# A graph layer and a gated feed-forward layer on one core: seven loads of weights and biases change their issuing engine and their place

## What is computed

```python
edge_index = jnp.stack([src, dst])          # 200000 edges, sorted by dst; 12500 nodes, 256 features
x = x + gnn(_layernorm(x), edge_index, W, att_src, att_dst, bias)
x = x + ffn(_layernorm(x)[None], mask, wr, br, w1, b1, w2, b2)[0]

def gnn(x, ...):                            # 4 heads of 64
    xp = (x @ W).reshape(n, H, C)
    a_src = einsum(xp, att_src); a_dst = einsum(xp, att_dst)
    alpha = leaky_relu(a_src[src] + a_dst[dst], 0.2)      # edges and self loops
    w = softmax of alpha over the edges of each dst
    return elu(segment_sum(xp[src] * w, dst) + bias)

def ffn(x, ...):                            # hidden width 1024
    weights = x @ wr + br;  pick the half of the rows with the largest weights
    y = (gelu(x[picked] @ w1 + b1) @ w2 + b2) * weights[picked]
    return x + y at the picked rows
```

## Time and profile before

| | us |
|---|---|
| median of 3 executions | 2301.69 |
| lowest and highest | 2298.26 and 2302.06 |
| the profiled execution | 2303.54 |
| its span in the profile | 2301.8 |

### The profile page before, as it was taken

The page is one execution under the profiler, slowest core; times in us unless marked ns, Lnnn a source line. Parts: engine busy times, 40 slices in busy tenths (PEclk is TensorE's granted clock), DMA queues, the critical chain, the costliest instruction groups (busy, mean ns, idle before and its releaser), DMA issues.

```text
span 2301.8 us, 39185 instructions
## 1 busy us (share of the span) xinstructions
PE 1900.7 (83%) x10810; PEld 1660.8 (72%) x10811; DVE 1608.2 (70%) x3952; ACT 707.3 (31%) x1868; POOL 1592.7 (69%) x1675
## 2 busy tenths in 40 slices
PE   5955888888888988888889888888889888888881
PEld 4844777777777777777777777777778677777771
DVE  5756767667776776667666766777667677777668
ACT  3530323322332333223322332233323332333230
POOL 2257777777777777777777777777777777777700
PEclk9977898899899899999989989989999899999985
DMA  7745545555555555555555555555545555555458
GB/s 238 222 137 147 152 143 154 158 143 149 158 154 142 155 153 158 145 148 159 153 146 150 155 157 144 149 158 153 156 141 152 159 148 144 158 155 157 132 170 296
DMA packets 216112, 365.40 MB, mean 159 GB/s; under 512 B 62165, under 2 KB 151409, under 8 KB 216082
## 3 DMA queue, kind: packets, MB, share of 16 engines
q0 software_dynamic: 77488, 214.85, 33.8%
q1 hardware_dynamic: 121570, 134.31, 18.4%
q10 hardware_dynamic: 17024, 15.90, 2.0%
HBM read 326.04 MB, written 38.89 MB: 159 GB/s over the span
## 4 chain that ended last, share of the span: by engine, by line
POOL 55%; issue 23%; PE 8%; POOLq 6%; DVE 4%; DMA 2%; ACTq 1%; ACT 1%; SPq 0%; DVEq 0%
POOL rows L611 55%; POOLq L365 3%; PE ag_ps L800 3%; PE ag_ps L910 3%; DVE base L1398 2%; DMA rows<-node_rows,ends 2%; POOLq L627 2%; PE y_ps L891 1%; PE h_ps L878 0%; DVE rows L1210 0%; PE tr_ps L823 0%; PE xl_ps L823 0%; DMA steps_of_rows<-in_L_gnn_att_dst 0%; DVE st_b L1016 0%; ACTq L657 0%
## 5 line engine op out<-in xcount | busy, mean ns | idle before, releaser
L611 POOL DMA_INDIRECT rows<-node_rows,ends x1613 | 1552.5, 963 | 504.0 <-issue 489.8
L910 PE MATMUL ag_ps<-rows,oh 128*128 128x260 f32 x3322 | 914.9, 443 | 291.1 <-DVE rows L1210 291.1
L910 PEld LDWEIGHTS ag_ps<-rows,oh 128*128 128x128 f32 x3322 | 731.3, 224 | 444.8 <-issue 298.4
L1210 DVE TENSOR_TENSOR rows<-rows,xl_ps 128x768 f32<-128x768 f32 (+2 forms) x685 | 495.7, 793 | 38.5 <-ACT xl_ps L731 38.5
L878 PE MATMUL h_ps<-xnT,w1s 128*128 128x128 f32 x3136 | 366.8, 275 | 0.0
L878 PEld LDWEIGHTS h_ps<-xnT,w1s 128*128 128x128 f32 x3136 | 358.2, 192 | 11.2
L731 ACT ACTIVATE xl_ps<-diff 128x68 f32<-128x68 f32 x98 | 22.6, 231 | 1109.9 <-DVE diff L1199 1099.4
L891 PE MATMUL y_ps<-w2s,hT 128*128 128x256 f32 x1568 | 359.6, 383 | 3.2 <-ACT hT L713 3.2
L1191 DVE TENSOR_TENSOR zz<-rows,edge_dm 128x68 f32<-128x68 f32 x98 | 22.4, 229 | 470.6 <-DMA rows<-node_rows,ends 373.2
L891 PEld LDWEIGHTS y_ps<-w2s,hT 128*128 128x128 f32 x1568 | 299.9, 192 | 45.2 <-issue 3.5
L1172 DVE TENSOR_TENSOR oh<-xl_ps,dloc 128x2176 f32<-128x2176 f32 x98 | 236.9, 2418 | 0.0
(11 more groups left out here) (183 smaller groups left out, 1329.6 us busy)
## 6 DMA issues: line engine op xcount, KB each, us to landing
dbc<-dst SPq DMA_DIRECT2D x97, 544.0 KB, 4.9
rows<-node_rows,ends POOLq DMA_INDIRECT x1613, 2.7
selfr<-node_rows SPq DMA_DIRECT2D x98, 130.0 KB, 2.1
base<-in_x SPq DMA_DIRECT2D x14, 896.0 KB, 5.2
base<-in_x SPq DMA_DIRECT2D x49, 256.0 KB, 2.8
ffn_rows<-yb ACTq DMA_DIRECT2D x96, 128.0 KB
node_rows<-base SPq DMA_DIRECT2D x13, 910.0 KB, 5.8
out<-base SPq DMA_DIRECT2D x3, 1024.0 KB, 6.1
```

Of the source, the lines that this page charges most:

```text
L611: pool.indirect_dma_start(out=rows[:, b, t, :], out_offset=None, in_=table, in_offset=bass.IndirectOffsetOnAxis(ap=ends[:, b, t, 0:1], axi ...
L910: product = nc.tensor.matmul(ag_ps[b][:, 0:ROW], oh[:, b, t, :], rows[:, b, t, :], start=(t == 0), stop=False)
L1210: nc.vector.tensor_tensor(v, v, e, ALU.mult).then_inc(scaled[k], 1)
```

## The change

The seven issues leave ScalarE's stream, where they stood ahead of its first copy. They stand now in SP's stream, in `batch_io(10)`, behind the store of batch 9 and ahead of that of batch 10. Their order, shapes, destinations and semaphores are the same, and no wait is added ahead of them.

```diff
+            def load_weights():
+                sp.dma_start(bias_f[0], bc(b2, D)).then_inc(b2_ld, 16)
+                sp.dma_start(gbs[:, :], bc(gbias, D)).then_inc(w_ld, 16)
+                sp.dma_start(w1s[:, :, :], w1.rearrange("(c p) n -> p c n", p=P)).then_inc(w_ld, 16)
+                sp.dma_start(w2s[:, :, :], w2.rearrange("(c p) n -> p c n", p=P)).then_inc(w_ld, 16)
+                with nc.allow_non_contiguous_dma("a bias by column of the hidden layer"):
+                    sp.dma_start(b1s[:, :], b1.rearrange("(c p) -> p c", p=P)).then_inc(w_ld, 16)
+                sp.dma_start(wrs[:, :], bc(wr.rearrange("d o -> (d o)"), D)).then_inc(w_ld, 16)
+                sp.dma_start(brs[:, :], bc(br, 1)).then_inc(w_ld, 16)
...
                 if known(g, 1):
                     store_rows(g - 1, 1 - b)
+                if isinstance(g, int) and g == NB - DEEP:
+                    load_weights()
...
-            act.dma_start(bias_f[0], bc(b2, D)).then_inc(b2_ld, 16)
-            act.dma_start(gbs[:, :], bc(gbias, D)).then_inc(w_ld, 16)
-            act.dma_start(w1s[:, :, :], w1.rearrange("(c p) n -> p c n", p=P)).then_inc(w_ld, 16)
-            act.dma_start(w2s[:, :, :], w2.rearrange("(c p) n -> p c n", p=P)).then_inc(w_ld, 16)
-            with nc.allow_non_contiguous_dma("a bias by column of the hidden layer"):
-                act.dma_start(b1s[:, :], b1.rearrange("(c p) -> p c", p=P)).then_inc(w_ld, 16)
-            act.dma_start(wrs[:, :], bc(wr.rearrange("d o -> (d o)"), D)).then_inc(w_ld, 16)
-            act.dma_start(brs[:, :], bc(br, 1)).then_inc(w_ld, 16)
```

## The result

| | us |
|---|---|
| kernel before, median of 5 (2296.31 to 2302.06) | 2298.26 |
| changed kernel, median of 5 (2285.30 to 2288.71) | 2287.04 |
| ratio, with its 95% interval | 0.9942 (0.9932 to 0.9953) |
| forecast for the changed kernel | 2289.3 |

The changed kernel is faster: by the ratio 0.58%, by the two medians 11.2 us, which is 0.49%; both lie inside the interval. The forecast was 12.4 us, 0.54%. Two further executions of the kernel before brought its median down by 3.4 us against the three that the forecast started from, so the gain is a little smaller than forecast while the time is 2.3 us lower. The profiled execution of the kernel before (2303.54 us) lies 5.3 us above that median. Measured again beside the first group of experiments, the same kernel has a ratio of 0.9947 (0.9933 to 0.9961), 11.6 us.

What follows compares the result with a forecast made beforehand. Stage two's GpSimd gathers fill over half the chain; the first waits for stage one's last table store. Terms -12.4 and 0 took 2303.54 to 2291.1 us, less 1.85 to the median: 2289.3 us, range 2285 to 2294.

Steps and rivals of the forecast that it cites:

- The main term: Front of stage one: without the seven issues on ScalarE, TensorE's first product comes at about 14.5 us, not 26.91; -12.4 us.
- D: Rival, chance 0.04: transfers pace the start, so moving the issues wins only their own 3.2 us; 2298.5 us.
- A: Rival, chance 0.09: the 6.12 us hold follows the 127 pieces and falls on ScalarE's copy; gain 9.4 us, 2292.3 us.
- cost nothing: Behind the first product: batch 1's normalization, target conversion, later loads and the moved loads on SP delay nothing; 0 us.
- the cover of batch 1: VectorE's normalized tiles, coming since 21.8 us, are ready before TensorE needs them at 25.3 us; about 3.5 us of cover.
- Loads of later batches are issued by the progress of the work itself and move with it.: Loads behind batch 3's were claimed to come earlier along with the work, at no cost.
- The clock: 0: TensorE's first products, 3.05 us lost to slow running, were taken to stay as slow after the change; gain 0.
- C: Rival, chance 0.05: TensorE's clock comes up sooner at its first products, winning up to 3.05 us more; 2286.3 to 2288 us.
- The price on SP: Seven issues behind batch 9's store take 3.4 to 15.5 us, taken towards the lower; term 0, range 0 to +1.5 us.
- B: Rival, chance 0.08: SP is held long and its queue is full, delaying batch 10's store; 2291 to 2292.5 us.
- E: Rival, chance 0.02: SP held some 53 us or more makes the last table stores late; at 55 us, about 2308 us.
- a microsecond of stage one shows up in the total: Stage one lies wholly ahead of the first gather, so each microsecond on its chain counts in the total if nothing gives it back.

Runs made afterwards that it cites:

- first group of experiments: The changed kernel, unaltered, measured again as the base for that group's other kernels: 2288.95 us, ratio 0.9947 to the kernel before.
- third group: The last set of executions, all programs some 900 us longer; its base, the changed kernel unaltered: 3225.46 us, ratio 0.9972 to the kernel before.

## Why the prediction was right, and where it was not

**The reading of the bound was right.** The first gather waits for the last store before and after. The main term too: the first copy was held by the seven issues. It was forecast to start at 14.0 us and started at 13.55, the first product at 14.07 for 14.5. Of that 0.36 us is an earlier landing of the attention vector in this execution (the first issue stands at 9.52 us, not 9.88). Term -12.4, measured -12.84. That SP issues from the same early place give most of the gain rules D out. A is out since in the changed kernel the copy starts 0.03 us after its tile is ready (12.86 + 0.66 = 13.52 us), 3.1 us behind the issue of the 127 pieces.

**The step that failed: "cost nothing" for everything behind the first product.** By the prediction's own sign (a new idle time of TensorE on VectorE's normalization before 40 us) this part is wrong. Two of its terms failed, the cover of batch 1 and the time of the store of batch 0.

*The cover at batch 1.* The prediction gave 3.5 us; by its own lead it was 0.9, and in this profile there was none. It took the mean of 3.97 us for each of the seven and had the first tile ready at 21.8 us, but the first operation was 2.0 us long and the others 0.4, so the tile was ready at 22.9 us. It also had TensorE come for it at 25.3 us, behind the seventh product, though the transposes of the eighth tile stand ahead of that product: by the forecast's lead at 36.24 - 12.4 = 23.8 us, and with the fast first steps of this profile at 22.05, where it waited 0.90 us. This wait cost next to nothing against the kernel before, which waits 0.84 us at this place for ScalarE's conversion of the targets: the eighth product is 38.57 - 24.33 = 14.24 us ahead, the ninth 39.78 - 25.44 = 14.34, as the fourth was (33.12 - 18.77 = 14.35).

*"Loads of later batches are issued by the progress of the work itself and move with it."* This was wrong for one load. The load of batch 5 waits for the normalization of batch 1, which VectorE does in its own time: its issue is at 25.26 us before and 24.90 us after. The store of batch 0 moved from 38.87 to 25.39 us and so came to stand 0.5 us behind it, in the same queue. It took 9.1 us to land, against 4.2 before, and ScalarE waited 1.89 us at batch 2, a term that the prediction did not have; in this pair of profiles 1.11 us of the lead were lost there.

**The clock: 0 is not refuted, and it is not shown.** In the pair of profiles above 1.5 us were won in TensorE's first three steps, which looks like the prediction's C. The other profiles take that back. With the change or a variant of it the three steps took 4.70, 4.69, 5.95, 5.63, 5.95, 5.46, 4.92, 5.74 and 5.04 us. Without it, behind the long wait, they took 6.21 us in the kernel before and 29.85 - 25.04 = 4.81 us with the 127 pieces moved. The two ranges lie over each other, so no gain by C is shown. TensorE idles for some 10 us ahead of its first transposes in either kernel, and only products put into a wait made the first tile fast (1.06 to 1.13 us for four).

These two findings are not independent. Where the first steps were fast, ScalarE waited for the store of batch 0; where they were slow (5.95 us, changed kernel of the third group), it came later and did not wait. The store of batch 2 was issued at 41.57, 41.94 and 41.63 us in the three profiles of the changed kernel, with first steps of 4.70, 4.69 and 5.95 us: what fast steps win, the wait takes back.

**The price on SP was right in effect and wrong in size.** The prediction took a value towards 3.4 us and named 3.4 to 8 us; the seven took 10.3 us. The outer bounds of 3.4 and 15.5 us held. The reason given, that the DMA engines are idle there (0.02), was read from a stretch of the kernel before, without the weights. With them the share was 0.86 from 97 to 101 us and 0.99 from 101 to 107. SP alone did not pay the lower bound either, so two queues that hold each other up are not the whole cause of the hold. With b1 last the longest hold fell to 1.5 us at a share of 0.82 to 0.85, so most of it belongs to the issue that follows the pieces of b1; how much the full engines add is not separated. The store of batch 10 was issued at 107.52 us, 0.5 us behind forecast and some 1.3 us behind the 106.2 at which it would have been due, and landed in 6.1 us; ScalarE's first copy of batch 12 waited only for TensorE, as before. B and E, which needed a late store there, did not happen. That the other stores follow "at least 10 us apart" was misread (in the kernel before the last ones are 7.8, 5.7 and 3.3 us apart), without effect.

**The sum** of 12.4 us came out as 13.7 us at the first gather: +0.4 in the first term, +1.5 in TensorE's first steps (by the spread just told), nothing net for batch 1, -1.1 at batch 2, +0.5 at the last store. By the medians it is 11.2 and 11.6 us. So the step "a microsecond of stage one shows up in the total" is shown only within some 2 us. They can lie in stage two, which varies by more than that, or in the single profile of the kernel before, whose stage one may not be typical; the record doesn't tell which. That the forecast comes so near is in part luck: errors of either sign in stage one cancel, and 2289.3 us started from a median 3.4 us too high. The measured 2287.04 us lies outside the 2288 to 2291 us that the prediction gave as its main case and inside those of C, which no run shows.

## What to carry to other kernels

An issue of a transfer costs its engine what the queue makes of it and not only what it transfers (the load of b2 took 6.12 us in the kernel before and 0.37 at ScalarE's batch 10), so it belongs on an engine for which nobody waits: here that alone gave 8.7 of 11.6 us, and a later place on the busy engine 4.7. A stretch that is idle before a change says little about how idle it is once the moved work stands in it. When work moves ahead, list every issue whose time does *not* move with it, and look for pairs that now meet in one queue. And read the members of a group of operations one by one where the first of them is what the next engine waits for.

## What was not expected of the hardware

- One GpSimd operation (L576, 2.85 us) stretched a VectorE operation of 0.4 us that ran beside it to 2.0 us.
- A store of 910 KB issued 0.5 us behind a load of 896 KB landed after 9.1, 9.4 and 9.5 us in three profiles; issued 2.7 us behind it, with the seven issues shortly ahead in the same queue, after 9.4 us; issued ahead of it, after 5.3 us; with no load near it, in the kernel before, after 4.2. Where it was issued 0.86 us behind (changed kernel, third group), the trace gives no landing; ScalarE came 8.85 us after the issue and did not wait, so it landed within that. How the landing depends on the distance stays open.
- A load of 1024 pieces of four bytes takes its issuing engine 0.6 to 5.5 us, and the issue behind it 3.8 to 6.1 us, at the start and at batch 10. With it last of the seven the longest hold was 1.5 and 2.0 us in two profiles.
- After a wait of 12.6 us TensorE took 2.10 us for four products and three tiles to come down to 1.06, after 11.35 us of waiting in another profile two tiles, and without such a wait behind its first transposes two or three tiles as well; kept at work with unused products it took 1.06 to 1.13 from the first. The granted clock shows as 1.00 in all these stretches. In the experiment with the issues at ScalarE's batch 10 it shows as 0.50 and the same four products take 2.13 us, so it is likely, though not shown, that the first products ran at the lower level (1.2 GHz) too.
- The time from the first gather to the end differed by 4.3 us between six profiles of nearly the same program, a third of the effect that was to be measured. The first gather of the changed kernel lay within 0.7 us in its three profiles, which makes the milestones of stage one the finer measure; the kernel before has one profile only.
